# Causal attention of two layers: scores and value products in one rotation of four PSUM banks, value products in two stretches, score-row banks released head by head

## Chip, cores, metric

One core of one Trainium2 chip. The metric is the device time of one execution in microseconds. Engines are called TensorE (PE in the profile; PEld is its weight load), VectorE (DVE), ScalarE (ACT), GpSimd (POOL) and SyncE (SP).

## What is computed

Two transformer layers on x of 4 x 512 x 256, 16 heads of 16 channels. Each layer has a causal attention and a feed-forward part. The change touches the core of the two attentions only, which one function emits for both:

```python
scores = einsum('bqhd,bkhd->bhqk', q, k) * scale     # 4 x 16 x 512 x 512, causal mask
attn = softmax(scores, axis=-1)
out = einsum('bhqk,bkhd->bqhd', attn, v)             # layer 1 shares one k and one v among the heads
```

## The kernel before

`phase_attention` (L705) runs once for each layer, over 16 groups `G`. A group is one batch row and four heads. All matmuls are fp32; the trace shows each as two instructions. For a group there are four kinds of work.

**Row units** (`rows`, L753; VectorE, L816). TensorE computes scores with queries on the partitions, and VectorE reads them from PSUM with the mask added, and reduces them to the negated maximum of each row. A unit `u` of 0 to 5 is one or two query tiles (`ROWS`, L671) of two heads: 512 columns for u = 0 and 3, 256 for u = 1 and 2, 384 + 128 for u = 4 and 5. The two heads have PSUM banks of their own: a pair out of banks 4 to 7, so two pairs rotate (`row_bank`). One semaphore increment for the pair says that it is computed, one that it has been read. In the order of this rotation the maxima's transpose takes a turn of its own, with a whole pair.

**Maxima** (`maxT`, L767; VectorE, L822). TensorE transposes the maxima (four transposes) when the last row unit of the group has been read; VectorE adds them to q. The q_and_max tile is what the next kind reads.

**Transposed scores** (`scoresT`, L737; ScalarE, L838; GpSimd, L851). TensorE computes scores with keys on the partitions, six units of two heads, which are 512, 512, 384 + 128, 384 + 128, 256 and 256 columns a head. ScalarE takes the exponential of each head out of PSUM into the probs tile, GpSimd zeroes the masked half of the diagonal blocks. Heads rotate over three banks, 0 to 2 (`e_bank`): head n waits until head n-3 has been read (L742).

**Value products** (`pv`, L773; ScalarE copy, L829). Four key blocks with 512, 384, 256 and 128 query columns, each with four heads side by side in the output partitions, all in bank 3. The bank is copied once a group.

The order on TensorE is written out by hand (L786 to L801). A group has six steps k = 0 to 5. Step k issues for each of two heads (i = 0, 1) the transposed scores of unit k of group G, and the row unit that is nine units ahead: units 3, 4, 5 of G+1 at k = 0, 1, 2, and units 0, 1, 2 of G+2 at k = 3, 4, 5. The four matmuls of a step use the four 32-row parts of the array, and the columns of both kinds agree at each k. Behind k = 3 stand the transposes for G+1; behind k = 1, 2, 3 and 4 stands one key block each of the value products of G-1 (`PV_AT`). ScalarE copies bank 3 behind the exponentials of k = 5. Each engine works strictly through its own order; a wait holds what stands behind it.

## Time and profile before

| | |
|---|---|
| median of 3 runs | 1081.67 us (1080.73 to 1081.95) |
| span of the profiled execution | 1073.4 us |
| attention core, layer 0 | about 306 to 486 us of the span |
| attention core, layer 1 | about 763 to 943 us of the span |
| busy over the span | PE 86%, DVE 57%, ACT 43%, POOL 27% |

Ends of matmuls are modelled in the profile, so TensorE counts as busy through short waits. What TensorE does is better read from the starts of its instructions in the timeline, one step after the other, and compared with the same step where nothing holds it. "[0.63 <-PE psum L749]" behind a row is the time that the engine had been idle and what released it.

### The profile page before, as it was taken

The page shows a single profiled execution, that of the slowest core. Times are in us where ns is not written, and L with a number is a line of the kernel's source. Part 1 is how long each engine was busy: PE and PEld are TensorE (multiplying, and loading weights), DVE is VectorE, ACT ScalarE, POOL GpSimd, SP SyncE. Part 2 cuts the span into 40 slices and gives each one's busy share as a digit, 9 for nine tenths or more (in the row PEclk, how much of TensorE's full clock was granted, in tenths as well). Part 3 has the DMA queues.
Part 4 walks back from the last instruction along what each step waited for, and adds up shares of the span by engine and source line. Part 5 has one row for each costly group of instructions (what it writes and reads, how often), then busy time and mean ns, then how long its engine had stood idle before and what let it go on. Part 6 is the DMA issues. An engine that isn't in the chain of part 4 may idle for free. (4 is left out here: it accounts for less than half of the span.)

```text
span 1073.4 us, 21548 instructions
## 1 busy us (share of the span) xinstructions
PE 917.8 (86%) x7991; PEld 599.4 (56%) x7991; DVE 610.8 (57%) x2052; ACT 462.5 (43%) x1050; POOL 287.4 (27%) x538
## 2 busy tenths in 40 slices
PE   6865906899969999998999899969899999988874
PEld 3544906777735555546986355534365555467453
DVE  1873794555547777736333635450377777366354
ACT  2563602000005656663232876463256666645054
POOL 1770311455512333330001200000023333340535
PEclk9995556655558999999688999869789999998788
DMA  5055443412200432002000000000000000083461
GB/s 120 4 115 123 133 157 114 95 40 80 62 18 1 95 125 60 2 1 89 1 1 22 6 0 1 1 1 1 1 1 1 2 2 2 1 213 99 160 255 48
DMA packets 54432, 60.42 MB, mean 56 GB/s; under 512 B 9049, under 2 KB 40247, under 8 KB 54072
## 3 DMA queue, kind: packets, MB, share of 16 engines
q1 hardware_dynamic: 43976, 44.31, 15.5%
q10 hardware_dynamic: 7488, 6.85, 2.4%
q0 software_dynamic: 2864, 7.89, 2.1%
q8 instruction: 64, 1.05, 0.4%
q14 instruction: 40, 0.33, 0.1%
HBM read 29.75 MB, written 25.99 MB: 52 GB/s over the span
## 5 line engine op out<-in xcount | busy, mean ns | idle before, releaser
L816 DVE CUSTOM_DVE_ANT_0 l_masked_scores<-psum,mask_q_rows 128x384 bf16<-128x384 f32 (+3 forms) x512 | 225.0, 488 | 77.0 <-PE psum L763 76.2
L838 ACT ACTIVATE l_probs<-psum 128x512 f32<-128x512 f32 (+1 forms) x384 | 186.3, 527 | 150.7 <-PE psum L749 150.0
L851 POOL TENSOR_SCALAR_AFFINE_SELECT l_probs<-l_probs 128x256 f32<-128x256 f32 x256 | 101.0, 406 | 380.9 <-ACT l_probs L838 380.7
L763 PE MATMUL psum<-kb_heads,q_heads 32*128 32x384 f32 (+3 forms) x512 | 109.4, 510 | 10.7 <-DVE l_neg_max_rows L805 8.7
L763 PE MATMUL psum<-l_k_heads,l_q_heads 32*128 32x384 f32 (+3 forms) x512 | 109.4, 509 | 4.6 <-DVE l_neg_max_rows L805 2.7
L749 PE MATMUL psum<-l_q_and_max,l_k_heads 32*128 32x256 f32 (+3 forms) x512 | 112.4, 472 | 0.0
L749 PE MATMUL psum<-l_q_and_max,kb_heads 32*128 32x256 f32 (+3 forms) x512 | 112.3, 472 | 0.0
L781 PE MATMUL psum<-l_probs,rows_32k 128*32 128x512 f32 (+3 forms) x1024 | 97.6, 459 | 2.9 <-POOL l_probs L851 2.9
L749 PEld LDWEIGHTS psum<-l_q_and_max,l_k_heads 32*128 32x128 f32 x512 | 59.0, 188 | 52.0 <-ACT l_probs L838 42.4
L749 PEld LDWEIGHTS psum<-l_q_and_max,kb_heads 32*128 32x128 f32 x512 | 58.9, 188 | 52.0 <-ACT l_probs L838 42.3
L641 POOL TENSOR_TENSOR v_new_and_ones<-v_and_k_rows 32x128 f32<-32x128 f32 x128 | 54.8, 445 | 49.7 <-DVE v_and_k_rows L618 46.0
L763 PEld LDWEIGHTS psum<-kb_heads,q_heads 32*128 32x128 f32 x512 | 53.4, 199 | 21.0 <-DVE l_neg_max_rows L805 8.9
L590 PE MATMUL psum<-eye_and_state,kT 32*128 32x64 f32 x1024 | 62.6, 416 | 2.5 <-PEq L46 1.5
L763 PEld LDWEIGHTS psum<-l_k_heads,l_q_heads 32*128 32x128 f32 x512 | 53.3, 198 | 15.6 <-DVE l_neg_max_rows L816 6.3
L618 DVE TENSOR_TENSOR v_and_k_rows<-psum,own_columns 128x512 f32<-128x512 f32 x64 | 44.2, 691 | 30.4 <-PE psum L590 30.4
L590 PEld LDWEIGHTS psum<-eye_and_state,kT 32*128 32x128 f32 x1024 | 56.7, 317 | 8.0 <-issue 7.9
L838 ACT ACT_TABLE_LOAD x2 | 2.6, 1283 | 115.9 <-PEq L46 115.9
L456 PE MATMUL psum<-rows_32k,v_and_k_rows 128*32 128x128 f32 x448 | 18.5, 339 | 35.5 <-DMA rows_32k<-inverse_scratch 35.5
L597 PE MATMUL psum<-v_and_k_rows,kb_slot_rows 128*32 128x64 f32 x992 | 40.1, 311 | 6.5 <-DVE v_and_k_rows L618 6.5
L816 DVE DVE_READ_ACCUMULATOR2_ANT l_neg_max_rows<- 128x1 f32 x512 | 42.5, 83 | 0.0
L1970 POOL TENSOR_TENSOR x_rows<-x_rows,last_gamma_beta 128x256 f32<-128x256 f32 x16 | 11.6, 727 | 114.0 <-PE psum L1656 114.0
L781 PEld LDWEIGHTS psum<-l_probs,rows_32k 128*32 128x32 f32 x1024 | 21.8, 110 | 31.7 <-issue 19.2
(351 smaller groups left out, 1704.2 us busy)
## 6 DMA issues: line engine op xcount, KB each, us to landing
...
```

Of the source, the lines that this page charges most:

```text
L456: last = nc.tensor.matmul(ps[SLOT * j:SLOT * j + SLOT, u % 4, (2 * cc + q) * P:(2 * cc + q + 1) * P], g.VK[:, u % NP * 2 + cc, 4 * (2 * x ...
L590: last = nc.tensor.matmul(ps[:, 4 * f + j, WB * q:WB * (q + 1)], UW[r, 2 * f + q, c, :], IS[r, f, q, :, :].rearrange("p b e -> p (b e)"), ...
L597: last = nc.tensor.matmul(ps[SLOT * j:SLOT * j + SLOT, 4 * f, 2 * WB + WB * q:2 * WB + WB * (q + 1)], g.KBP[:, c, 4 * (2 * f + q) + j, :], ...
L618: nc.vector.tensor_tensor(VA[:, s % NV, f, :, :, :, :].rearrange("p j q b e -> p j q (b e)"), ps[:, 4 * f:4 * f + 4, 0:2 * WB].rearrange(" ...
L641: last = nc.gpsimd.tensor_tensor(out[:, f, :, :, :], v0, v1, ALU.add)
L749: mm = nc.tensor.matmul(ps[:, e_bank(G, u, i), o:o + w], KT(b, gq)[r, kb * P:(kb + 1) * P], QM[r, G % 2, kb * P:N], start=True, stop=True)
L763: mm = nc.tensor.matmul(ps[:, row_bank(G, u, i), o:o + w], QT(b, gq)[r, t * P:(t + 1) * P], KT(b, gq)[r, 0:w], start=True, stop=True)
L781: last = nc.tensor.matmul(ps[SLOT * j:SLOT * j + SLOT, PV_BANK, kb * P:N], va(b, kb, 4 * gq + j), PT[:, G % 2, j, o:o + w], start=(kb == 0 ...
L816: last = nc.vector.tensor_tensor_reduce(out=junk[:, ROW_AT[G, u] % 2, i, o:o + w], in0=ps[:, row_bank(G, u, i), o:o + w], in1=g.maskq[:, N ...
L838: nc.scalar.activation(PT[:, G % 2, 2 * (u % 2) + i, o:o + w], ps[:, e_bank(G, u, i), 0:w], ACT.Exp, scale=SCALE).then_inc(x_ok, 1)
L851: last = nc.gpsimd.affine_select(out=d, in_=d, pattern=[[0, 2], [1, P]], compare_op=ALU.is_ge, fill=0.0, base=0, channel_multiplier=-1)
L1970: nc.gpsimd.tensor_tensor(g.X[:, c, :], g.X[:, c, :], g.gb_last[:, 1, :], ALU.add).then_inc(xb_ok, 1)
```

## The change

- `row_bank`: each head of a row unit has its own turn in a rotation of four banks, and its own increments on both semaphores. A head waits for the read of the fourth turn before it. The transposes take one turn, not two. VectorE goes head by head.
- `e_bank`: the score heads and the value products share a rotation of four banks, 0 to 3. A group has 14 turns: k0 (two), k1 (two), value product 0, k2, k3, value product 1, k4, k5. Each waits for the read of the fourth turn before it.
- `pv`: two stretches, by query halves. The first, behind k = 1, has queries 0 to 255 (256 and 128 columns of key blocks 0 and 1). The second, behind k = 3 and the transposes, has queries 256 to 511 (256, 256, 256 and 128 columns of the key blocks 0 to 3). That makes six blocks in place of four, with the same sum of 1280 columns a head. The first waits for the masks of four units only, the second for all six.
- The ScalarE copy is two copies of 256 columns, each right behind the exponentials of k = 1 and of k = 3.
- The nine row units that run ahead of group 0 stand in one loop; the transposes of group 0 come behind the sixth, not the seventh.

```diff
--- before.py
+++ after.py
@@ -671,22 +671,37 @@
 ROWS = [[(3, 0)], [(1, 0)], [(1, 0)], [(3, 0)], [(2, 0), (0, 384)], [(2, 0), (0, 384)]]
 UNITS = 6
 PTW = 1280
-PV_AT = {1: [(0, 0)], 2: [(1, 512)], 3: [(2, 1024)], 4: [(3, 896)]}
-
-
-def row_units(G, k):
-
-    n = (G + 1, k + 3) if k < 3 else (G + 2, k - 3)
-    return [n] if 0 <= n[0] < NGRP else []
-
-
-ROW_ORDER = []
-for _G in range(-2, NGRP):
+PT_AT = [0, 512, 1024, 896]
+PV_TURNS = [(1, 0, 256), (3, 256, 512)]
+LEAD = 9
+MAXT_AT = 3
+PV_NEEDS = [max(u for u in range(UNITS) for kb, _ in KEYS[u // 2] if kb * P < q1) + 1 for _, q0, q1 in PV_TURNS]
+
+
+def row_unit(n):
+
+    return [(n // UNITS, n % UNITS)] if n < UNITS * NGRP else []
+
+
+SCORE_AT, ROW_AT, UNIT_AT = {}, {}, {}
+for _n in range(LEAD):
+    for _i in range(2):
+        ROW_AT[_n // UNITS, _n % UNITS, _i] = len(ROW_AT)
+    if _n == UNITS - 1:
+        ROW_AT[0, UNITS, 0] = len(ROW_AT)
+for _G in range(NGRP):
     for _k in range(UNITS):
-        ROW_ORDER += row_units(_G, _k)
-        if _k == 3 and 0 <= _G + 1 < NGRP:
-            ROW_ORDER.append((_G + 1, UNITS))
-ROW_AT = {n: i for i, n in enumerate(ROW_ORDER)}
+        for _i in range(2):
+            SCORE_AT[_G, _k, _i] = len(SCORE_AT)
+            for _H, _u in row_unit(LEAD + UNITS * _G + _k):
+                ROW_AT[_H, _u, _i] = len(ROW_AT)
+        if _k == MAXT_AT and _G + 1 < NGRP:
+            ROW_AT[_G + 1, UNITS, 0] = len(ROW_AT)
+        for _x, _t in enumerate(PV_TURNS):
+            if _t[0] == _k and _G:
+                SCORE_AT[_G - 1, UNITS, _x] = len(SCORE_AT)
+for _x in range(len(PV_TURNS)):
+    SCORE_AT[NGRP - 1, UNITS, _x] = len(SCORE_AT)
 
 
 def load_heads(eng, g, b):
@@ -711,17 +726,16 @@
...
-        junk = sb("masked_scores", [P, 2, 2, N], BF16)
-        zero_ok, row_ps, row_ok = sem("max_rows_zeroed"), sem("score_rows_psum"), sem("row_unit_done")
-        e_ps, x_ok, p_ok, pv_ok, ot_sb = (sem("scoresT_psum"), sem("exponentials"), sem("masked_probs"), sem("pv_done"), sem("out_group_sbuf"))
+        junk = sb("masked_scores", [P, 4, N], BF16)
+        zero_ok, row_ps, row_ok = sem("max_rows_zeroed"), sem("score_rows_psum"), sem("score_rows_read")
+        e_ps, x_ok, p_ok, pv_ok = sem("scoresT_psum"), sem("score_bank_read"), sem("masked_probs"), sem("pv_done")
         block = ctx.enter_context(nc.Block())
-        PV_BANK = 3
 
         def e_bank(G, u, i):
-            return (2 * UNITS * G + 2 * u + i) % 3
+            return SCORE_AT[G, u, i] % 4
 
         def row_bank(G, u, i):
-            return 4 + 2 * (ROW_AT[G, u] % 2) + i
+            return 4 + ROW_AT[G, u, i] % 4
 
...
-                n = 2 * UNITS * G + 2 * u + i
                 if part == 0:
-                    if n >= 3:
-                        pe.wait_ge(x_ok, n - 2)
+                    if SCORE_AT[G, u, i] >= 4:
+                        pe.wait_ge(x_ok, SCORE_AT[G, u, i] - 3)
                     if u == 0 and i == 0:
-                        pe.wait_ge(row_ok, ROW_AT[G, UNITS] + 1)
+                        pe.wait_ge(row_ok, ROW_AT[G, UNITS, 0] + 1)
...
             def rows(G, u, i, part):
                 b, gq, j = G // HG, G % HG, 2 * (u % 2) + i
-                if part == 0 and i == 0:
-                    if ROW_AT[G, u] >= 2:
-                        pe.wait_ge(row_ok, ROW_AT[G, u] - 1)
-                    if streamed and u == 0 and gq == 0:
+                if part == 0:
+                    if ROW_AT[G, u, i] >= 4:
+                        pe.wait_ge(row_ok, ROW_AT[G, u, i] - 3)
+                    if streamed and u == 0 and i == 0 and gq == 0:
                         pe.wait_ge(g.heads_ld[b], 16 * (5 if b else 6))
...
-                if part == len(ROWS[u]) - 1 and i == 1:
+                if part == len(ROWS[u]) - 1:
                     mm.then_inc(row_ps, 1)
 
             def maxT(G):
-                pe.wait_ge(row_ok, max(ROW_AT[G, UNITS] - 1, ROW_AT[G, UNITS - 1] + 1))
+                pe.wait_ge(row_ok, max(ROW_AT[G, UNITS, 0] - 3, ROW_AT[G, UNITS - 1, 1] + 1))
                 for t in range(4):
                     last = nc.tensor.transpose(ps[:, row_bank(G, UNITS, 0), t * P:(t + 1) * P], mx[:, G % 2, t, :], g.idf[:, :])
                 last.then_inc(row_ps, 1)
 
-            def pv(G, kb, o):
+            def pv(G, x):
                 b, gq = G // HG, G % HG
-                if kb == 0:
-                    pe.wait_ge(p_ok, 2 * UNITS * (G + 1))
-                    if G:
-                        pe.wait_ge(ot_sb, G)
-                w = N - kb * P
-                for j in range(4):
-                    last = nc.tensor.matmul(ps[SLOT * j:SLOT * j + SLOT, PV_BANK, kb * P:N], va(b, kb, 4 * gq + j), PT[:, G % 2, j, o:o + w], start=(kb == 0), stop=(kb == 3))
-                if kb == 3:
-                    last.then_inc(pv_ok, 1)
+                _, q0, q1 = PV_TURNS[x]
+                pe.wait_ge(p_ok, 2 * UNITS * G + 2 * PV_NEEDS[x])
+                pe.wait_ge(x_ok, SCORE_AT[G, UNITS, x] - 3)
+                blocks = [kb for kb in range(4) if kb * P < q1]
+                for kb in blocks:
+                    lo = max(q0, kb * P)
+                    o = PT_AT[kb] - kb * P
+                    for j in range(4):
+                        last = nc.tensor.matmul(ps[SLOT * j:SLOT * j + SLOT, e_bank(G, UNITS, x), lo:q1], va(b, kb, 4 * gq + j), PT[:, G % 2, j, o + lo:o + q1],
+                                                start=(kb == 0), stop=(kb == blocks[-1]))
+                last.then_inc(pv_ok, 1)
+
+            def step(S, row):
+                for part in range(2):
+                    for i in range(2):
+                        for G, u in S:
+                            if part < len(KEYS[u // 2]):
+                                scoresT(G, u, i, part)
+                        for G, u in row:
+                            if part < len(ROWS[u]):
+                                rows(G, u, i, part)
 
             pe.wait_ge(zero_ok, 1)
-            for G in range(-2, NGRP):
+            for n in range(LEAD):
+                step([], row_unit(n))
+                if n == UNITS - 1:
+                    maxT(0)
+            for G in range(NGRP):
                 for k in range(UNITS):
-                    for part in range(2):
-                        for i in range(2):
-                            if G >= 0 and part < len(KEYS[k // 2]):
-                                scoresT(G, k, i, part)
-                            for rG, ru in row_units(G, k):
-                                if part < len(ROWS[ru]):
-                                    rows(rG, ru, i, part)
-                    if k == 3 and 0 <= G + 1 < NGRP:
+                    step([(G, k)], row_unit(LEAD + UNITS * G + k))
+                    if k == MAXT_AT and G + 1 < NGRP:
                         maxT(G + 1)
-                    for kb, o in PV_AT.get(k, []):
-                        if G >= 1:
-                            pv(G - 1, kb, o)
-            for kb, o in ((0, 0), (1, 512), (2, 1024), (3, 896)):
-                pv(NGRP - 1, kb, o)
+                    for x, turn in enumerate(PV_TURNS):
+                        if turn[0] == k and G:
+                            pv(G - 1, x)
+            for x in range(len(PV_TURNS)):
+                pv(NGRP - 1, x)
 
         @block.vector
         def _(dve):
             nc.vector.memset(mx[:, :, :, :], 0.0).then_inc(zero_ok, 1)
             dve.wait_ge(zero_ok, 1)
-            for n, (G, u) in enumerate(ROW_ORDER):
+            for n, (G, u, i) in enumerate(ROW_AT):
                 b, gq = G // HG, G % HG
                 dve.wait_ge(row_ps, n + 1)
                 if u < UNITS:
-                    h0 = 2 * (u % 2)
+                    c = SLOT * (2 * (u % 2) + i) + max_row
                     for t, o in ROWS[u]:
                         w = (t + 1) * P
-                        for i in range(2):
-                            out = mx[:, G % 2, t, SLOT * (h0 + i) + max_row:SLOT * (h0 + i) + max_row + 1]
-                            last = nc.vector.tensor_tensor_reduce(out=junk[:, ROW_AT[G, u] % 2, i, o:o + w], in0=ps[:, row_bank(G, u, i), o:o + w], in1=g.maskq[:, N - w:N], scale=-1.0,
-                                                                  scalar=3.0e38, op0=ALU.add, op1=ALU.min, accum_out=out)
+                        last = nc.vector.tensor_tensor_reduce(out=junk[:, n % 4, o:o + w], in0=ps[:, row_bank(G, u, i), o:o + w], in1=g.maskq[:, N - w:N], scale=-1.0,
+                                                              scalar=3.0e38, op0=ALU.add, op1=ALU.min, accum_out=mx[:, G % 2, t, c:c + 1])
                     last.then_inc(row_ok, 1)
                 else:
                     if G >= 2:
@@ -823,22 +844,18 @@
 
         @block.scalar
         def _(act):
-            def out_group(G):
+            for n, (G, u, i) in enumerate(SCORE_AT):
                 b, gq = G // HG, G % HG
-                act.wait_ge(pv_ok, G + 1)
-                nc.scalar.copy(OT[:, gq, :, R * b:R * b + R], ps[:, PV_BANK, :].rearrange("p (c i) -> p c i", c=NT)).then_inc(ot_sb, 1)
-
-            for G in range(NGRP):
-                for u in range(UNITS):
-                    for i in range(2):
-                        act.wait_ge(e_ps, 2 * UNITS * G + 2 * u + i + 1)
-                        if u == 0 and i == 0 and G >= 2:
-                            act.wait_ge(pv_ok, G - 1)
-                        o, w = SPAN[u // 2]
-                        nc.scalar.activation(PT[:, G % 2, 2 * (u % 2) + i, o:o + w], ps[:, e_bank(G, u, i), 0:w], ACT.Exp, scale=SCALE).then_inc(x_ok, 1)
-                    if u == 5 and G:
-                        out_group(G - 1)
-            out_group(NGRP - 1)
+                if u < UNITS:
+                    act.wait_ge(e_ps, 2 * UNITS * G + 2 * u + i + 1)
+                    if u == 0 and i == 0 and G >= 2:
+                        act.wait_ge(pv_ok, len(PV_TURNS) * (G - 1))
+                    o, w = SPAN[u // 2]
+                    nc.scalar.activation(PT[:, G % 2, 2 * (u % 2) + i, o:o + w], ps[:, e_bank(G, u, i), 0:w], ACT.Exp, scale=SCALE).then_inc(x_ok, 1)
+                else:
+                    _, q0, q1 = PV_TURNS[i]
+                    act.wait_ge(pv_ok, len(PV_TURNS) * G + i + 1)
+                    nc.scalar.copy(OT[:, gq, q0 // R:q1 // R, R * b:R * b + R], ps[:, e_bank(G, UNITS, i), q0:q1].rearrange("p (c i) -> p c i", i=R)).then_inc(x_ok, 1)
 
         @block.gpsimd
         def _(pool):
@@ -846,7 +863,7 @@
                 for u in range(UNITS):
                     for part, (kb, o) in enumerate(KEYS[u // 2]):
                         if part == 0:
-                            pool.wait_ge(x_ok, 2 * UNITS * G + 2 * u + 2)
+                            pool.wait_ge(x_ok, SCORE_AT[G, u, 1] + 1)
                         d = PT[:, G % 2, 2 * (u % 2):2 * (u % 2) + 2, o:o + P]
                         last = nc.gpsimd.affine_select(out=d, in_=d, pattern=[[0, 2], [1, P]], compare_op=ALU.is_ge, fill=0.0, base=0, channel_multiplier=-1)
                     last.then_inc(p_ok, 2)
```

## Rows read from the trace of the kernel before

**Rows 1.** Adds of maxima to q of layer 0: min/median/max ns, first and last start (us).
```profile
L822 DVE TENSOR_TENSOR l_q_and_max<-q_heads,psum x16: 681/682/689, 319.9 to 468.7; 128x512 f32<-128x512 f32 x16
```

**Rows 2.** Busy time by window: each engine's busy us (instructions), granted clock, DMA share, GB/s.
```profile
440.00:450.00 10.00, 10.00 (x104) 5.53 (x103) 7.78 (x34) 6.19 (x13) 3.26 (x10) 1.00 0.00 0
```

**Rows 3.** Timeline, TensorE, one period: start, duration in us, line, out<-in, shape, count.
```profile
440.44 0.43 PE L781 MATMUL psum<-l_probs,rows_32k 128*32 128x128 f32 x8
440.80 0.48 PE L749 MATMUL psum<-l_q_and_max,kb_heads 32*128 32x256 f32 x1
...
441.34 0.59 PE L749 MATMUL psum<-l_q_and_max,kb_heads 32*128 32x512 f32 x1
...
441.97 0.69 PE L749 MATMUL psum<-l_q_and_max,kb_heads 32*128 32x512 f32 x1
...
442.46 0.58 PE L763 MATMUL psum<-kb_heads,q_heads 32*128 32x384 f32 x1
...
443.22 0.69 PE L749 MATMUL psum<-l_q_and_max,kb_heads 32*128 32x512 f32 x1
...
444.29 1.06 PE L781 MATMUL psum<-l_probs,rows_32k 128*32 128x512 f32 x8
445.28 0.59 PE L749 MATMUL psum<-l_q_and_max,kb_heads 32*128 32x384 f32 x1
...
446.36 0.85 PE L781 MATMUL psum<-l_probs,rows_32k 128*32 128x384 f32 x8
447.14 0.59 PE L749 MATMUL psum<-l_q_and_max,kb_heads 32*128 32x384 f32 x1
...
448.22 0.66 PE L770 MATMUL psum<-identity,l_neg_max_rows 128*128 128x128 f32 x4
448.80 0.64 PE L781 MATMUL psum<-l_probs,rows_32k 128*32 128x256 f32 x8
449.37 0.69 PE L749 MATMUL psum<-l_q_and_max,kb_heads 32*128 32x256 f32 x2
449.71 0.48 PE L763 MATMUL psum<-kb_heads,q_heads 32*128 32x256 f32 x1
```

**Rows 4.** Timeline, ScalarE, the same period.
```profile
441.53 0.66 ACT L838 ACTIVATE l_probs<-psum 128x256 f32<-128x256 f32 x2 [0.59 <-PE psum L749]
442.07 0.59 ACT L829 COPY l_heads_out<-psum 128x512 f32<-128x512 f32 x1
442.54 1.67 ACT L838 ACTIVATE l_probs<-psum 128x512 f32<-128x512 f32 x3
```

**Rows 5.** Timeline, VectorE, the same period.
```profile
440.60 0.42 DVE L816 CUSTOM_DVE_ANT_0 l_masked_scores<-psum,mask_q_rows 128x256 bf16<-128x256 f32 x1 [0.25 <-PE psum L763]
...
441.29 0.08 DVE L816 DVE_READ_ACCUMULATOR2_ANT l_neg_max_rows<- 128x1 f32 x1
...
446.55 0.56 DVE L816 CUSTOM_DVE_ANT_0 l_masked_scores<-psum,mask_q_rows 128x384 bf16<-128x384 f32 x1 [0.63 <-PE psum L763]
...
447.93 0.08 DVE L816 DVE_READ_ACCUMULATOR2_ANT l_neg_max_rows<- 128x1 f32 x1
...
449.57 0.08 DVE L816 DVE_READ_ACCUMULATOR2_ANT l_neg_max_rows<- 128x1 f32 x1
```

**Rows 6.** Timeline, TensorE, the last group of layer 0.
```profile
470.15 3.54 PE L749 MATMUL psum<-l_q_and_max,kb_heads 32*128 32x256 f32 x12
...
481.28 3.94 PE L781 MATMUL psum<-l_probs,rows_32k 128*32 128x512 f32 x28 [1.31 <-POOL l_probs L851]
```

**Rows 7.** Busy time and granted clock of one window in the tail of layer 0.
```profile
482.00:483.00 1.00, 1.00 (x12) 0.36 (x8) 0.00 (x0) 0.00 (x0) 0.00 (x0) 0.50 0.09 16
```

**Rows 8.** Timeline, ScalarE, the last copy of layer 0.
```profile
485.39 0.58 ACT L829 COPY l_heads_out<-psum 128x512 f32<-128x512 f32 x1 [4.26 <-PE psum L781]
```

**Rows 9.** Timeline, TensorE, the start of layer 0's attention.
```profile
318.64 1.12 PE L770 MATMUL psum<-identity,l_neg_max_rows 128*128 128x128 f32 x4
...
321.67 1.06 PE L749 MATMUL psum<-l_q_and_max,kb_heads 32*128 32x512 f32 x1
```

## The prediction

> **What bounds the kernel now.** I read the table of line groups first, for which engine waits for which, then the busy time of one window, then the timeline of one whole period engine by engine. The program repeats itself: the adds of the maxima to q run from 319.9 to 468.7 us, 16 of them, 9.92 us apart [rows 1]. Layer 1 has the same shape, so the two attentions are 32 groups, some 318 us. In a window of 10 us at full clock VectorE is busy for 7.78 us and ScalarE for 6.19 [rows 2]. Neither fills the period, and TensorE's "busy" hides its waits, so its starts must be compared step by step.
>
> The starts in order give these lengths [rows 3]: value block of 128 columns 0.36, k5 0.54, k0 1.16 (441.34 to some 442.5), k1 1.8, value block of 512 columns 0.99, k2 1.08, block of 384 columns 0.78, k3 1.08, transposes 0.58, block of 256 columns 0.57, k4 0.97. The sum is 9.90. Three of them are longer than the work in them:
> - The second head of k0 starts at 441.97, 0.6 behind the first. With three banks it waits for the exponential of k5's first head, which started at 441.53 [rows 4].
> - The second head of k1 starts at 443.22, when the exponential of k0's first head is read. That one stood behind the 512-column copy of 442.07 and ran from 442.54, 0.59 long [rows 4].
> - k4 is issued at 449.37, but its row matmul starts at 449.71. It waits for VectorE's last read of the pair of k3, which ended at 449.65 [rows 5]; the transposes' turn had taken the other pair of banks. From the end of a read to the start of what it frees, then, 0.06.
>
> So the period is bound by no engine but by rounds from TensorE to ScalarE or VectorE and back, through too few banks.
>
> **What the change does to each term.**
>
> *Value products.* Four stretches of 128, 256, 384 and 512 columns take 0.36, 0.57, 0.78 and 0.99 [rows 3]: 0.21 for each 128 columns and 0.15 once a stretch. The new first stretch has 384 columns: 0.78. The second has 896: 7 x 0.21 + 0.15 = 1.62. Together 2.40 for 2.70. The eight more block matmuls of a group are costed at nothing, since the four heads' loads lie beside streaming matmuls. If each of the two added blocks pays the 0.15 of a stretch again it is 0.3 more a group, which is the bound from above.
>
> *ScalarE.* The exponential of a head may now be read up to four turns later, and the copy is half as wide (0.38 at most, as two 256-column exponentials take 0.66 [rows 4]) and stands behind k1 and k3. For k0 only the exponentials of k4 are needed. The first starts 0.73 after its matmuls (440.80 to 441.53), the second ends 0.66 later [rows 3, 4], with 0.06 for the release 1.45 after the start of k4. k4 and k5 back to back take 2 x 0.54 = 1.08. ScalarE would hold k0's second head for 0.37, less than VectorE does below. k1 needs the exponentials of k5, done before k0's first head has streamed. ScalarE leaves the path.
>
> *Row banks at k4.* The transposes take one turn. k4's heads need the reads of k2's second head and of k3's first, long done. The 0.34 of k4 goes.
>
> *Row banks at k0.* Here a wait comes in. Before, a value block stood between k4 and k5 and covered VectorE; now k4, k5 and k0 stand back to back, and k0's second head needs the read of k4's second head. k4's row matmuls start at 439.81 (449.71 less one period), VectorE starts on them at 440.60, 0.79 later, and has read both heads at 441.37, 0.77 later [rows 5]. A boundary between two units costs about 0.05 on VectorE now; going head by head adds such a boundary (taken as 0.05, bounds 0 and 0.1). With the release: 0.79 + 0.77 + 0.05 + 0.06 = 1.67 after the start of k4. TensorE is there at 1.08. The wait is **0.59**. What is queued behind it on TensorE is k1 and the first value stretch. k1's second head follows its forerunner in k0 by what one head takes, 1.03 (the head released at 441.43 is followed at 442.46 [rows 3, 5]), and the value stretch follows 1.07 behind that (443.22 to 444.29).
>
> *The transposes.* A second wait comes in. They need VectorE's reads of both heads of k2. Before, a value block of 0.78 lay between k2 and k3 and was their cover; now k2, k3 and the transposes stand back to back. VectorE starts on k2's rows 1.27 after the start of k2 (445.28 to 446.55), and its last read ends at 448.01, 1.46 later [rows 3, 5]. With 0.05 and 0.06 the transposes may start 2.84 after k2; TensorE is there at 2 x 1.08 = 2.16. The wait is **0.68**. Behind it stand the long value stretch, k4 and k5, which need nothing from it. VectorE is not late for k2: k1's rows take it 1.46 like k2's, k0's less, and there are 3.3 between the first head of k0 and k2 and 1.27 more.
>
> *The new period*, once around TensorE: k4 to k0's second head 1.67, to k1's second head 1.03, to the value stretch 1.07, that 0.78, k2 to the transposes 2.84, transposes 0.58, value stretch 1.62. **9.59** against 9.90, so 0.31 less. Without the two waits it would be 8.32. Fourteen groups of a layer are of this kind: 28 x 0.31 = 8.7 us.
>
> *The last group* has no rows, so neither wait of VectorE. From the start of k5 before it to the end of its own k5 it is now 470.15 to 479.97 (481.28 less an idle time of 1.31 [rows 6]), 9.82 us. After: 0.54 + 0.37 + 1.03 + 1.07 + 0.78 + 2.16 + 1.62 + 0.54 + 0.70 (a last step with its results) = 8.81. 1.0 less in each layer.
>
> *The tail.* Now all four blocks wait for the last mask. They start at 481.28, the clock granted is 0.50 of full (1.2 GHz) within them [rows 7], and the copy is done at 485.97 [rows 8]: 4.69 us. After, the first stretch runs while ScalarE and GpSimd finish, and only 896 columns and a half copy stand behind the mask: 1.62 + 0.1 + 0.38 = 2.1 at full clock, 3.6 at half. TensorE is idle for about 0.5 us less than before ahead of it, so I take full clock: 2.5 less in each layer, with 1.1 as the other end.
>
> *The start.* The transposes of group 0 come one row step earlier, so of the 3.0 us between them and the first transposed score [rows 9] one 512-column row step more stands behind them. 512 columns are 4 x 0.21 at full clock and twice that at half, so up to 1.7 more. Releases by single heads shorten the row steps before, where VectorE idles; from the 0.6 between heads up to 1.3 back. I take zero, from -1.3 to +1.7 in each layer.
>
> *Sum.* 8.7 + 2 x (1.0 + 2.5) = 15.7 us. The profiled execution spans 1073.4 us, 8.3 under the median; its new span is 1057.7, the time **1066** us.
>
> *A rule against it.* Row matmuls get six more semaphore increments a group. What hides them here is that transposed scores already have one for each head, and that the results of both heads are read one after the other. The Trainium skill (TensorE: Matmul & The Clock Gate, "The cost: per-tile semaphore tail") says that increments of concurrent tiles serialize, at about 26 ns each. By it an estimated 0.05 more stands in each of the two rounds, and the time would be 1069. No row of this trace separates it.
>
> **Rivals.**
> - *The waits are smaller than I price them.* A head's bank is given back after its own read, so TensorE may already load and stream the first head of a step while the second waits, and my chain of second heads may lose less than 0.59. For it: before, the two heads of k0 and k1 ran 0.6 apart and k1 did overlap k0. Against it: the value stretch behind k1 waits for both. With half of both waits gone, a period of 8.95: 28 x 0.95 + 7 = 34, so 1048 us.
> - *The new waits take all.* The added blocks pay 0.15 each and VectorE goes slower head by head (0.1 for a boundary); the period is 9.59 + 0.3 + 0.1, as before. Only the ends gain: 1075 us.
> - *Slower: the clock.* The wait before the transposes leaves the array idle for 0.68 in each group, where now the longest full stop of the two shown is about 0.2 (441.97 + 1.03 to 443.22 [rows 3]). In the tail the clock was at half after a stop of 1.31 [rows 6, 7]. If the clock fell after each transposes' wait, the value stretch would take 1.5 more and k4 and k5 0.85 more, 2.3 a group; in all groups 1130 us. It decides from 8 groups of 28 on (15.7 + 2.2 over 2.3). Against it: the stop is half of that in the tail, with dense work on both sides, and the clock is 1.00 in all full windows now.
>
> **How the numbers follow.** Forecast 0.55 (1060 to 1072), smaller waits 0.16, waits that take all 0.18, slower 0.11 by the clock or by a wait of this kind longer than 1.2. The range reaches half way into the fast case and over the third: 1047 to 1079. Some 0.2% can be told from no change, 2 us. The third case ends within that one time in four. Faster 0.84, within 0.05, slower 0.11.
>
> **What would show it.** In the profile after: adds of maxima 9.6 apart; no stop between k4's scores and rows; the second head of k0 about 0.6 behind where k5 ends, released by VectorE; transposes released by VectorE 2.84 after k2, and not by the end of k3; stretches of 0.78 and 1.62; exponentials that no longer hold TensorE; the last value stretch at full clock. It is wrong if the period is bound by ScalarE, if the stretches are longer, or if the granted clock falls inside groups.

## The result and the profile after

The changed kernel takes 1044.18 us (median of four runs, 1041.61 to 1046.53), the kernel before 1081.62 on the same chip (1080.73 to 1081.95). The ratio is 0.967, interval 0.964 to 0.970: 37 us less. The forecast of 1066 had the sign right and the size wrong; 1044 lies just under the range.

The profiled execution of the changed kernel spans 1043.1 us (1044.79 timed), 30.3 less than the 1073.4 of before. Where it went, each stretch read from first to last instruction, us per attention (layer 0 / layer 1):

| | before | after | saved, both | forecast |
|---|---|---|---|---|
| start of the attention to the first add of maxima | 13.7 / 13.6 | 12.8 / 12.5 | 2.0 | 0 |
| 15 periods between the 16 adds | 148.8 / 148.9 | 139.5 / 140.0 | 18.2 | 8.7 |
| last add to the first matmul of the next stage | 18.0 / 18.2 | 14.4 / 14.7 | 7.1 | 7.0 |
| whole attention | 180.5 / 180.7 | 166.7 / 167.2 | 27.3 | 15.7 |
| everything outside the two | 712.3 | 709.2 | 3.1 | 0 |

The adds of the maxima to q, grouped by line, give the period; the two numbers behind "686, " and "687, " are the first and last start in each layer:

```profile
L843 DVE TENSOR_TENSOR l_q_and_max<-q_heads,psum x16: 682/682/686, 318.1 to 457.6; 128x512 f32<-128x512 f32 x16
L843 DVE TENSOR_TENSOR l_q_and_max<-l_q_heads,psum x16: 681/682/687, 759.4 to 899.4; 128x512 f32<-128x512 f32 x16
```

(457.6 - 318.1) / 15 = 9.30 us, against 9.92 [rows 1]. This mean takes in the first two gaps and the last, which differ; each of the twelve between them is 9.27 here and 9.90 before. Below, "adds ... apart" is the mean of all 15 gaps, and "period" is one of the twelve. Three line groups of the page of the changed kernel show what happened to the two other engines: us busy and mean ns of one, then the idle time ahead of them and its main cause.

```profile
L837 DVE CUSTOM_DVE_ANT_0 l_masked_scores<-psum,mask_q_rows 128x128 bf16<-128x128 f32 (+3 forms) x512 | 220.0, 488 | 60.2 <-PE psum L776 60.2
L854 ACT ACTIVATE l_probs<-psum 128x512 f32<-128x512 f32 (+1 forms) x384 | 171.7, 530 | 75.9 <-PE psum L762 75.8
...
L858 ACT COPY l_heads_out<-psum 128x256 f32<-128x256 f32 x64 | 23.9, 374 | 59.1 <-PE psum L796 57.7
```

ScalarE's exponentials waited 150.7 us for scores before and wait 75.9 now; its copies waited 8.7 for value products and wait 59.1, so a good part of the waiting only moved to the copies. The row reads of VectorE (L837) waited 77.0 and wait 60.2. Which engine holds TensorE is read from the timeline.

One period of TensorE, from the timeline of the changed kernel (start, length, line, form, in brackets idle time and who ended it). L762 are transposed scores, L776 row scores, L783 the transposes of maxima, L796 value products:

```profile
419.84 0.66 PE L783 MATMUL psum<-identity,l_neg_max_rows 128*128 128x128 f32 x4 [0.71 <-DVE l_neg_max_rows L837]
420.43 1.72 PE L796 MATMUL psum<-l_probs,rows_32k 128*32 128x256 f32 x32
422.08 0.48 PE L762 MATMUL psum<-l_q_and_max,kb_heads 32*128 32x256 f32 x1
...
423.52 0.69 PE L762 MATMUL psum<-l_q_and_max,kb_heads 32*128 32x512 f32 x1
423.69 0.69 PE L776 MATMUL psum<-kb_heads,q_heads 32*128 32x512 f32 x1
...
424.65 0.67 PE L762 MATMUL psum<-l_q_and_max,kb_heads 32*128 32x512 f32 x2
...
425.08 0.59 PE L762 MATMUL psum<-l_q_and_max,kb_heads 32*128 32x512 f32 x1
...
425.60 0.86 PE L796 MATMUL psum<-l_probs,rows_32k 128*32 128x256 f32 x16
426.38 0.58 PE L762 MATMUL psum<-l_q_and_max,kb_heads 32*128 32x384 f32 x1
...
429.11 0.66 PE L783 MATMUL psum<-identity,l_neg_max_rows 128*128 128x128 f32 x4 [0.71 <-DVE l_neg_max_rows L837]
```

And the reads of VectorE that stand behind them:

```profile
422.85 0.42 DVE L837 CUSTOM_DVE_ANT_0 l_masked_scores<-psum,mask_q_rows 128x256 bf16<-128x256 f32 x1 [1.25 <-PE psum L776]
...
423.55 0.08 DVE L837 DVE_READ_ACCUMULATOR2_ANT l_neg_max_rows<- 128x1 f32 x1
...
427.59 0.56 DVE L837 CUSTOM_DVE_ANT_0 l_masked_scores<-psum,mask_q_rows 128x384 bf16<-128x384 f32 x1 [0.36 <-PE psum L776]
...
428.97 0.08 DVE L837 DVE_READ_ACCUMULATOR2_ANT l_neg_max_rows<- 128x1 f32 x1
```

Both new waits are there. The transposes at 429.11 come 0.71 idle after k3, when the last read of k2's second head is done (428.97 + 0.08 = 429.05). The second head of k0 issues its rows at 423.69, when the last read of k4's second head is done (423.55 + 0.08 = 423.63), with its bank the one released. ScalarE still holds the scores of k0's second head: they are issued at 423.52, as soon as the exponential of k4's second head has read its bank, 1.44 after k4 (the forecast had 1.45). VectorE's hold ends 0.17 later and is the one that counts. So ScalarE is close behind: by these rows a faster VectorE at this place alone would gain an estimated 0.17 a period at most. The forecast's terms beside these rows:

| once around TensorE | forecast | measured | from |
|---|---|---|---|
| k4 to rows of k0's second head | 1.67 | 1.61 | 422.08, 423.69 |
| that to the first value stretch | 1.03 + 1.07 | 1.91 | 423.69, 425.60 |
| first stretch | 0.78 | 0.78 | 425.60, 426.38 |
| k2 to transposes | 2.84 | 2.73 | 426.38, 429.11 |
| transposes | 0.58 | 0.59 | 419.84, 420.43 |
| second stretch | 1.62 | 1.65 | 420.43, 422.08 |
| sum | 9.59 | 9.27 | |

In the tail, the last value stretch and the copy behind it (timeline), and one window (columns: window, length, busy us and count on TensorE, its loads, VectorE, ScalarE, GpSimd, then granted clock, DMA share, GB/s):

```profile
469.11 1.72 PE L796 MATMUL psum<-l_probs,rows_32k 128*32 128x256 f32 x32 [0.41 <-POOL l_probs L868]
470.90 0.37 ACT L858 COPY l_heads_out<-psum 128x256 f32<-128x256 f32 x1 [1.77 <-PE psum L796]
```

```profile
469.00:470.00 1.00, 0.89 (x16) 0.55 (x20) 0.00 (x0) 0.12 (x1) 0.06 (x1) 1.00 0.06 16
```

The last stretch starts after 0.41 of idle (0.70 in layer 1), runs at full clock and takes 1.7; before, the blocks started after 1.31 of idle and fell to half clock [rows 6, 7].

### The profile page after: what moved, and what is told of

The parts are those of the page before. It is cut to its first block and busy times, and to the rows that moved or that the text cites. A ratio compares the mean times of both kernels' runs of the same rounds, so it can differ in the third digit from the quotient of the medians.

```text
span 1043.1 us, 22638 instructions
## 1 busy us (share of the span) xinstructions
PE 862.9 (83%) x8503; PEld 611.2 (59%) x8503; DVE 605.0 (58%) x2052; ACT 459.4 (44%) x1082; POOL 288.2 (28%) x538
## 5 line engine op out<-in xcount | busy, mean ns | idle before, releaser
L837 DVE CUSTOM_DVE_ANT_0 l_masked_scores<-psum,mask_q_rows 128x128 bf16<-128x128 f32 (+3 forms) x512 | 220.0, 488 | 60.2 <-PE psum L776 60.2
L854 ACT ACTIVATE l_probs<-psum 128x512 f32<-128x512 f32 (+1 forms) x384 | 171.7, 530 | 75.9 <-PE psum L762 75.8
L776 PE MATMUL psum<-kb_heads,q_heads 32*128 32x384 f32 (+3 forms) x512 | 93.5, 488 | 10.4 <-DVE l_neg_max_rows L828 8.7
L776 PE MATMUL psum<-l_k_heads,l_q_heads 32*128 32x384 f32 (+3 forms) x512 | 93.8, 492 | 4.4 <-DVE l_neg_max_rows L828 2.7
L762 PE MATMUL psum<-l_q_and_max,l_k_heads 32*128 32x384 f32 (+3 forms) x512 | 91.6, 462 | 0.0
L762 PE MATMUL psum<-l_q_and_max,kb_heads 32*128 32x384 f32 (+3 forms) x512 | 90.9, 457 | 0.0
L796 PE MATMUL psum<-l_probs,rows_32k 128*32 128x256 f32 (+1 forms) x1536 | 82.5, 347 | 1.1 <-POOL l_probs L868 1.1
L776 PEld LDWEIGHTS psum<-kb_heads,q_heads 32*128 32x128 f32 x512 | 58.9, 197 | 18.0 <-DVE l_neg_max_rows L828 8.9
L776 PEld LDWEIGHTS psum<-l_k_heads,l_q_heads 32*128 32x128 f32 x512 | 59.5, 198 | 12.0 <-DVE l_neg_max_rows L837 3.9
L762 PEld LDWEIGHTS psum<-l_q_and_max,l_k_heads 32*128 32x128 f32 x512 | 56.1, 189 | 17.8 <-issue 6.1
L796 PEld LDWEIGHTS psum<-l_probs,rows_32k 128*32 128x32 f32 x1536 | 43.6, 109 | 38.5 <-issue 8.5
L762 PEld LDWEIGHTS psum<-l_q_and_max,kb_heads 32*128 32x128 f32 x512 | 54.9, 186 | 17.8 <-issue 6.0
L858 ACT COPY l_heads_out<-psum 128x256 f32<-128x256 f32 x64 | 23.9, 374 | 59.1 <-PE psum L796 57.7
L837 DVE DVE_READ_ACCUMULATOR2_ANT l_neg_max_rows<- 128x1 f32 x512 | 42.6, 83 | 0.0
```

Source lines behind the costliest of these rows:

```text
L762: mm = nc.tensor.matmul(ps[:, e_bank(G, u, i), o:o + w], KT(b, gq)[r, kb * P:(kb + 1) * P], QM[r, G % 2, kb * P:N], start=True, stop=True)
L776: mm = nc.tensor.matmul(ps[:, row_bank(G, u, i), o:o + w], QT(b, gq)[r, t * P:(t + 1) * P], KT(b, gq)[r, 0:w], start=True, stop=True)
L796: last = nc.tensor.matmul(ps[SLOT * j:SLOT * j + SLOT, e_bank(G, UNITS, x), lo:q1], va(b, kb, 4 * gq + j), PT[:, G % 2, j, o + lo:o + q1], ...
L837: last = nc.vector.tensor_tensor_reduce(out=junk[:, n % 4, o:o + w], in0=ps[:, row_bank(G, u, i), o:o + w], in1=g.maskq[:, N - w:N], scale ...
L854: nc.scalar.activation(PT[:, G % 2, 2 * (u % 2) + i, o:o + w], ps[:, e_bank(G, u, i), 0:w], ACT.Exp, scale=SCALE).then_inc(x_ok, 1)
L858: nc.scalar.copy(OT[:, gq, q0 // R:q1 // R, R * b:R * b + R], ps[:, e_bank(G, UNITS, i), q0:q1].rearrange("p (c i) -> p c i", i=R)).then_i ...
```

## The experiments

My theory after the result: the period is closed by two rounds from TensorE to VectorE and back, k4 to k0 and k2 to the transposes, and only the head times inside them were priced too high. Rivals: the row banks alone give the gain; the score banks alone do; VectorE's sheer load (7.7 us in a period of 9.3) is the limit; the gain comes from smaller stretches and not from the shared banks; the clock.

**Both kernels once more**, for the spread between executions.

> The kernel before, profiled once more. Its medians lie 37.4 us above those of the changed kernel, the two profiled spans only 30.3 apart (1073.4 and 1043.1), while in the changed kernel time less span is 1.7. Theory: the first profiled execution of before was a short one by some 6 us, outside the attentions, and a new profile spans 1078 to 1080 with the same period of 9.9 us in the attentions. Rival: the difference is in the attentions, and the adds of the maxima lie more than 9.92 us apart here.

> The changed kernel once more, on the same chip as the others of this call: period 9.27 us, each attention 166.7 to 167.3 us from its first VectorE instruction to the next stage's first matmul; the time anywhere from 1036 to 1047, since the stages outside the attentions differ by several us between executions and chips.

Kernel before: median 1079.03 of ten (1065.62 to 1084.09), ratio 1.0012 (0.9967 to 1.0057). Its profile spans 1077.1 where the first one spanned 1073.4. The period is 9.90 again, layer 1 takes 180.6, and the rest, everything outside the two attentions, 711.3 (712.3 in the first profile). Layer 0 takes 185.2 instead of 180.5: from its last add to the next stage it is 23.3, not 18.0. So the time between the two profiles does not lie outside the attentions, as was expected, but in the last group of layer 0. TensorE there, in the first profile and then in this one:

```profile
473.63 1.07 PE L781 MATMUL psum<-l_probs,rows_32k 128*32 128x512 f32 x8
```

```profile
474.55 1.79 PE L781 MATMUL psum<-l_probs,rows_32k 128*32 128x512 f32 x8
...
487.00 4.50 PE L781 MATMUL psum<-l_probs,rows_32k 128*32 128x512 f32 x32 [1.31 <-POOL l_probs L851]
```

The granted clock falls to 0.50 at some 475 us, within the last group, while in the first profile it fell at 481 us, where the last value products start. Nothing in the order of the work differs.

The changed kernel: 1044.62, ratio 0.9655 (0.9581 to 0.9729), period 9.27, attentions 167.1 and 166.2 (expected were 166.7 to 167.3; the start of layer 1 is 0.7 shorter), rest 709.1. Its tails repeat to 0.01 us.

**The row banks by heads, alone.** The kernel before with its row banks given and taken back head by head; score banks, value products and order as before (its waits and increments by heads are left out here).

```diff
-            ROW_ORDER.append((_G + 1, UNITS))
+            ROW_ORDER.append((_G + 1, UNITS, 0))
-            return 4 + 2 * (ROW_AT[G, u] % 2) + i
+            return 4 + ROW_AT[G, u, i] % 4
```

> Before, with only the row banks given back head by head (the transposes take one turn). Theory: only the wait of 0.34 us at k4 goes, since the two other waits are for ScalarE; the period falls from 9.90 to about 9.55, some 0.9 less at each start: 1081.6 - 28 x 0.35 - 2 = about 1070. Rival (what holds one head holds all; ScalarE's waits take up whatever the rows give): period 9.85 or more, time within 3 us of before.

1059.68 us, ratio 0.9836 (0.9785 to 0.9887). Adds 9.49 and 9.52 apart. The period is 9.57, 0.33 less, and the wait of k4 that goes was 0.34 [rows 3]: the theory of 9.55 holds. The tail is as before (17.9 and 18.3). The time is 17 us under the kernel before on the same chip (1076.79), where some 12 were expected, so the row banks alone give about half of the saving.

**The other half, alone.** The changed kernel with row banks in pairs again: one release for a unit, and the transposes take a pair's turn (the waits and increments by pairs are left out here).

```diff
-            return 4 + ROW_AT[G, u, i] % 4
+            return 4 + 2 * (ROW_AT[G, u] % 2) + i
```

> The changed kernel, with the row banks as before: pairs, one increment a pair, the transposes with a pair's turn. Theory: the new period of 9.27 us is made by the score banks and the two stretches; rows by pairs delay k0's first head to 1.67 us after k4 too, but the second follows without a gap, so the period is 9.3 to 9.4 and the time 1046 to 1050. Rival (the release by heads carries the gain that the forecast missed): period 9.6 as forecast, 1053 to 1056.

1054.14 us, ratio 0.9792 (0.9726 to 0.9858). The tail is 14.4 and 14.7, as in the changed kernel: the tail belongs to the value stretches. The timeline of one period, TensorE:

```profile
421.12 0.58 PE L761 MATMUL psum<-l_q_and_max,kb_heads 32*128 32x384 f32 x1
...
426.14 0.48 PE L761 MATMUL psum<-l_q_and_max,kb_heads 32*128 32x256 f32 x1
...
427.31 0.69 PE L761 MATMUL psum<-l_q_and_max,kb_heads 32*128 32x512 f32 x1
427.81 0.69 PE L775 MATMUL psum<-kb_heads,q_heads 32*128 32x512 f32 x1
...
430.52 0.58 PE L761 MATMUL psum<-l_q_and_max,kb_heads 32*128 32x384 f32 x1
```

Period 430.52 - 421.12 = 9.40. Here k0 (its first scores at 427.31) has both row heads behind the read of both heads of k4: rows at 427.81, 1.67 after k4 at 426.14. In the changed kernel only the second head waits, at 1.61, while the first is already streaming. The period was expected at 9.3 to 9.4 and found at 9.40; the time was expected at 1046 to 1050 and missed. Off the period: 0.33 by the rows alone, 0.50 by the rest alone, 0.63 by both. They don't add: in the changed order the transposes and the long stretch stand before k4, and k4's rows follow its scores at once with pairs too (426.14 and 426.15), so both halves take away the same 0.34 of k4; on top of the rest, heads in place of pairs give 0.13.

**Is VectorE's read of k2 on the path, or its load?** One more read of VectorE, 0.48 us of work on constants in SBUF whose result nobody uses, once between the two reads of k2's rows, once at another place of the same period, behind the add of the maxima.

```diff
# dve_more_k2, in the loop over row heads
+                    if u == 5 and i == 1:
+                        nc.vector.tensor_tensor_reduce(out=spare[:, :], in0=g.maskq[:, 0:384], in1=g.maskq[:, 0:384], ...)
# dve_more_idle, behind the add to q
+                    nc.vector.tensor_tensor_reduce(out=spare[:, :], in0=g.maskq[:, 0:384], in1=g.maskq[:, 0:384], ...)
```

> The changed kernel with one more 384-column read and reduction on VectorE (of a constant in SBUF, its result unused) in each group, ahead of the last reads of k2's second head: about 0.48 us. Theory (the transposes wait for these reads): period 9.27 + 0.48 = 9.75. Rival (VectorE has 1.5 us of slack a period and the wait is hidden in the array's streaming): 9.27 to 9.35.

> The same additional read, but behind the add of the maxima to q, where VectorE then waits for k4's rows for 1.2 us. Theory: period unchanged at 9.27. Rival (VectorE's own load binds): 9.75 as in the other place.

1056.64 and 1045.57 us (one run each). With the read in k2 the adds are 9.81 apart and the period is 9.75, 0.48 more than 9.27, as expected. Timeline of VectorE, then of TensorE, from that kernel:

```profile
425.72 0.55 DVE L837 CUSTOM_DVE_ANT_0 l_spare<-mask_q_rows 128x384 bf16<-128x384 f32 x1
...
426.89 0.08 DVE L840 DVE_READ_ACCUMULATOR2_ANT l_neg_max_rows<- 128x1 f32 x1
```

```profile
427.03 0.66 PE L784 MATMUL psum<-identity,l_neg_max_rows 128*128 128x128 f32 x4 [1.19 <-DVE l_neg_max_rows L840]
```

The spare read runs at 425.72, the last read of k2 ends at 426.97, and the transposes start at 427.03 after 1.19 of idle instead of 0.71. With the same work behind the add, VectorE's timeline of the other kernel:

```profile
420.29 0.56 DVE L838 CUSTOM_DVE_ANT_0 l_masked_scores<-psum,mask_q_rows 128x384 bf16<-128x384 f32 x1 [0.36 <-PE psum L777]
...
423.50 0.55 DVE L845 CUSTOM_DVE_ANT_0 l_spare<-mask_q_rows 128x384 bf16<-128x384 f32 x1
...
424.83 0.42 DVE L838 CUSTOM_DVE_ANT_0 l_masked_scores<-psum,mask_q_rows 128x256 bf16<-128x256 f32 x1 [0.77 <-PE psum L777]
...
429.56 0.56 DVE L838 CUSTOM_DVE_ANT_0 l_masked_scores<-psum,mask_q_rows 128x384 bf16<-128x384 f32 x1 [0.36 <-PE psum L777]
```

From k2's first read to the next, 429.56 - 420.29 = 9.27, as without it: the wait before k4's reads (424.83) shrank from 1.25 to 0.77 and took all of it. The same 0.48 costs 0.48 in one place and nothing in the other. (The adds are 9.37 apart there in the mean, since the second of the 15 gaps grew by 0.5.) VectorE's load is not the limit, and its round at k2 is. That its round at k4 is one too is read from the starts and from the moves below; no read was added there.

**Moving the value stretches.** If a round is what counts, a stretch put into it should cover it. Four placements, all by two numbers:

```diff
-PV_TURNS = [(1, 0, 256), (3, 256, 512)]
+PV_TURNS = [(1, 0, 256), (4, 256, 512)]   # pv_k1_k4
+PV_TURNS = [(2, 0, 256), (3, 256, 512)]   # pv_k2_k3
+PV_TURNS = [(2, 0, 256), (4, 256, 512)]   # pv_k2_k4
+PV_TURNS = [(1, 0, 256), (4, 256, 512)]   # max_k4_pv_k4, with
+MAXT_AT = 4
```

> The changed kernel with the second value stretch behind k4, not behind the transposes. Theory of two waits for VectorE on the path: the stretch of 1.65 us now covers VectorE's reads of k4, the wait of 0.5 us at k0 goes (0.1 may come back at k5 or k1), the wait of 0.7 before the transposes stays: period 8.8 to 8.9, 1044 - 28 x 0.4 = about 1033. Rival (the array's own streaming binds, waits are hidden in it): period within 0.1 of 9.27, time within 3 us of the changed kernel.

1044.26 us, ratio 0.9682 (0.9627 to 0.9738); adds 9.16. The long stretch now lies between k4 and k5 and covers VectorE's reads of k4. TensorE and the read that ends its new wait:

```profile
423.86 0.48 PE L762 MATMUL psum<-l_q_and_max,kb_heads 32*128 32x256 f32 x1
...
425.46 0.60 PE L776 MATMUL psum<-kb_heads,q_heads 32*128 32x384 f32 x2
```

```profile
425.33 0.08 DVE L837 DVE_READ_ACCUMULATOR2_ANT l_neg_max_rows<- 128x1 f32 x1
```

k5 starts at 423.86. Now k5, k0 and k1 stand back to back, and k1's second head needs the read of k5's second head, which ends at 425.41: its rows go at 425.46, 1.60 after k5. The wait moved by one step. The forecast of 8.8 to 8.9 had missed it; the period is 9.07, 0.2 less than the changed kernel's. The time is not less (1033 was expected): the attentions are 165.1 and 165.3, 3.5 us less together, but the rest of the profiled execution is 717.2 where the changed kernel had 709.2.

> The changed kernel with the first value stretch behind k2, not k1. Theory: the stretch of 0.79 us covers VectorE's reads of k2, so the wait of 0.7 before the transposes goes; but k2 then follows k1 at once and its second head needs the read of k0's, some 0.3 later than it could start: period about 8.9, transposes released by the end of k3 and not by VectorE. Rival (no wait before the transposes is on the path): period 9.27 or more.

Adds 9.03 apart, one run, 1045.21 us. TensorE:

```profile
419.09 0.48 PE L762 MATMUL psum<-l_q_and_max,kb_heads 32*128 32x256 f32 x1
...
425.80 0.66 PE L783 MATMUL psum<-identity,l_neg_max_rows 128*128 128x128 f32 x4
...
428.03 0.48 PE L762 MATMUL psum<-l_q_and_max,kb_heads 32*128 32x256 f32 x1
```

With the short stretch between k2 and k3, the transposes follow k3 at 425.80 with no idle time: VectorE reads k2 under the stretch and k3. Period 428.03 - 419.09 = 8.94, 0.33 less than 9.27, as expected. From k2 to the transposes the changed kernel takes 2.73, and k2 and k3 without a stop take 2.16: 0.57 went there, and 0.24 of it came back at k2, which now follows k1 at once.

> The changed kernel with the transposes and the second value stretch both behind k4. Theory (two rounds to VectorE are left on the path): the 0.7 us before the transposes are filled by k4 (0.54 us of work), the round of k4 by the stretch; what stays is VectorE's round from k5 to k1, 1.6 us, as in the run with the stretch behind k4 alone. Sum: k5 to the first stretch 2.66, that 0.79, k2 to the transposes 2.73, transposes 0.59, stretch 1.65: period 8.42, 1044 - 28 x 0.85 = about 1020. Rival (VectorE's or ScalarE's own work binds below 9 us): period 8.9 or more, 1033 or more.

1039.83 us, ratio 0.9649 (0.9576 to 0.9722); adds 9.13 and 9.15. TensorE and the read:

```profile
427.00 0.48 PE L776 MATMUL psum<-kb_heads,q_heads 32*128 32x256 f32 x1
...
427.69 0.48 PE L776 MATMUL psum<-kb_heads,q_heads 32*128 32x256 f32 x1
```

```profile
427.55 0.08 DVE L837 DVE_READ_ACCUMULATOR2_ANT l_neg_max_rows<- 128x1 f32 x1
```

Expected was 8.42, found 9.04. Moving the transposes moves their turn among the four row banks. Now k4's second head gets the bank of k2's second head, whose read ends at 427.63: its rows go at 427.69, 0.69 after the first head's. The read of k2 that held the transposes holds k4 instead: from k2 to the transposes it is 3.35 (424.96 to 428.31) where 2.73 was expected, the whole 0.62.

> The changed kernel with the value stretches behind k2 and k4, the transposes behind k3 as they are: each stretch now stands where VectorE is behind. Theory: no wait before the transposes (as with the stretch behind k2), none of k4 at k0; what stays is VectorE's round from k5 to k1's second head (1.60 us, 0.3 of it waiting) and from k0's reads to k2 (about 0.4). Sum: k5 to the first stretch 4.07, that 0.79, k3 1.07, transposes 0.59, k4 0.65, stretch 1.65: period 8.8, 0.45 under the changed kernel, so about 13 us less than that kernel on the same chip. Rival (the wait moves and grows back, as it did with the transposes behind k4): 9.0 or more.

1043.17 us, ratio 0.9656 (0.9591 to 0.9721); adds 9.12. TensorE, and a read of VectorE:

```profile
420.49 0.48 PE L762 MATMUL psum<-l_q_and_max,kb_heads 32*128 32x256 f32 x1
...
420.75 0.48 PE L776 MATMUL psum<-kb_heads,q_heads 32*128 32x256 f32 x1
...
423.03 0.48 PE L762 MATMUL psum<-l_q_and_max,kb_heads 32*128 32x256 f32 x1
...
427.09 0.86 PE L796 MATMUL psum<-l_probs,rows_32k 128*32 128x256 f32 x16
```

```profile
420.62 0.08 DVE L837 DVE_READ_ACCUMULATOR2_ANT l_neg_max_rows<- 128x1 f32 x1
```

k5 (423.03) to the first stretch (427.09) takes 4.06, as expected. But k4 now follows the transposes with no long stretch between, and its second head has the bank of k3's first head. That read ends at 420.70; the rows go at 420.75, 0.26 after the first head. Expected 8.8, found 9.04.

Its tail is 0.5 longer than the changed kernel's, since the first stretch starts a step later. All four placements end between 8.94 and 9.07. In all four a part of the wait that was removed came back in the next step that takes the bank; in three of them more than was expected.

**Two stretches without the shared rotation.** Scores rotate through three banks and value products keep the fourth, as before; stretches, order and row banks as in the changed kernel.

```diff
-            return SCORE_AT[G, u, i] % 4
+            return 3 if u == UNITS else (2 * UNITS * G + 2 * u + i) % 3
```

> The changed kernel with three banks for the scores and the fourth for the value products alone, as before; stretches, copies and row banks as changed. It tells the shared rotation from the rest. Theory: with three banks ScalarE holds k0's second head until 1.17 us after k5, 0.1 longer than VectorE does, and k1's second head until the exponential of k0's first is read, 0.26 longer: period 9.6. Rival (the gain is in the stretches and rows, since VectorE's waits cover ScalarE's anyway): 9.27 to 9.35.

1073.69 us, adds 10.19 apart, period 10.21: slower in its groups than the kernel before (9.90). TensorE, then ScalarE:

```profile
429.06 0.81 PE L763 MATMUL psum<-l_q_and_max,kb_heads 32*128 32x384 f32 x2
...
429.89 0.58 PE L763 MATMUL psum<-l_q_and_max,kb_heads 32*128 32x384 f32 x1
```

```profile
429.24 1.08 ACT L856 ACTIVATE l_probs<-psum 128x512 f32<-128x512 f32 x2 [0.66 <-PE psum L763]
```

The second head of k3 issues at 429.89, 0.83 behind the first, when the exponential that started at 429.24 has read its bank. With one bank fewer, ScalarE stands on the path again, at k3, k5 and k1. I had expected 9.6 and counted only k5 and k1; three stops add up to more. The fourth bank in the rotation is worth 10.21 - 9.27 = 0.94 us a period in this order, more than the whole gain of 0.63; cutting the value products in two without it loses 0.31 against the kernel before. The time is still under that of the kernel before on the same chip (1078.66), though the attentions are longer (184.2 and 182.0): the rest of its one execution took 705.8.

**The tail.** In the last group alone, both value stretches wait for the last mask.

```diff
-                pe.wait_ge(p_ok, 2 * UNITS * G + 2 * PV_NEEDS[x])
+                pe.wait_ge(p_ok, 2 * UNITS * G + 2 * (UNITS if G == NGRP - 1 else PV_NEEDS[x]))
```

> The changed kernel, but the first value stretch of the last group of each layer also waits for the last mask, as all value products did before. From the last add of the maxima to the next stage it is 14.4 and 14.7 us in the changed kernel, 18.0 and 18.2 before. Theory of the tail (the early stretch saves its own 0.8, and more by keeping the clock up): 2.4 us of matmuls behind the mask at half clock are 4.8, so 14.4 + 0.8 + 2.4 = 17.6. Rival (the clock stays up, only the length counts): 15.2.

1050.36 us. Periods as in the changed kernel. The tail is 15.1 in layer 0 and 17.0 in layer 1, for 14.4 and 14.7: the rival in layer 0 (15.2), near the theory in layer 1 (17.6). TensorE in both, and the window of layer 1:

```profile
471.41 2.37 PE L796 MATMUL psum<-l_probs,rows_32k 128*32 128x256 f32 x48 [1.28 <-POOL l_probs L868]
...
913.76 4.05 PE L796 MATMUL psum<-l_probs,rows_32k 128*32 128x256 f32 x48 [1.57 <-POOL l_probs L868]
```

```profile
915.00:916.00 1.00, 1.00 (x16) 0.49 (x12) 0.00 (x0) 0.33 (x1) 0.00 (x0) 0.50 0.00 0
```

The same 48 block matmuls take 2.37 us after a stop of 1.28, and 4.05 after one of 1.57, with the granted clock at 0.50 (1.2 GHz). So of the 3.6 that the tail and the last group gain in each layer, 0.7 is the first stretch done early, and 1.7 more is the clock where it falls. That the shorter stop is what keeps the clock at full is not shown. In the run with three banks it fell to 0.50 in layer 0 within the last stretch, after a stop of 0.58:

```profile
486.89 3.05 PE L798 MATMUL psum<-l_probs,rows_32k 128*32 128x256 f32 x32 [0.58 <-ACT l_heads_out L860]
```

The same stretch of layer 1, after the same stop of 0.58, ran at full clock in 1.72. And in the second profile of the kernel before it fell at 475 us with no stop of TensorE longer than 0.1 us in the 40 us ahead of it. The length of the last stop alone does not decide it.

## Why the prediction was right and wrong

- *Where the 37 us lie.* The forecast was 15.7, so it is off by 21.7. Of this 11.6 is in the attentions (9.5 in the periods, 2.0 at the start, 0.1 in the tail), 3.1 in what lies outside them, which the forecast put at nothing, and 7.0 in the base (below). With the attentions alone, 27.3 us less, the time would have been 1054. The step of the prediction that failed is the sum for the new period, 9.59 for a measured 9.27; its mechanism stands, and its terms were too large.
- *What bounds it* was right. No engine is full; the old stops of k0, k1 and k4 are gone. ScalarE is off the path by 0.17 only, as the forecast had it (1.44 for 1.45 behind k4).
- *The two new waits* were right in place and cause: 0.71 before the transposes for a forecast of 0.68, and k0's second head released 1.61 after k4 for 1.67. Doing k2's read 0.48 later cost 0.48.
- *The term that failed most: k0 to the first stretch.* I took 1.03 for a head and 1.07 from the head to the stretch, both from rows in which a second head had been held: within the 1.03 (441.43 to 442.46 [rows 3]) ScalarE held k0's second head, and the 1.07 starts at 443.22, where k1's second head was released. With k1's heads following without a stop, 1.91 is what both take, for 2.10. That is 0.19 of the 0.32 a period. Some 0.11 of it shows in k1's second head: its two passes of scores start 0.54 apart in the kernel before (443.22 and the row below) and 0.43 apart here (424.65, 425.08). The other 0.08 no row separates.

```profile
443.76 0.59 PE L749 MATMUL psum<-l_q_and_max,kb_heads 32*128 32x512 f32 x1
```

- *The 0.05 for a boundary between heads on VectorE* was nothing. The two reads of k2 take 1.46 (427.59 to 429.05) as before, those of k4 0.78 for 0.77. And VectorE starts 1.21 after k2, not 1.27: it no longer waits for the second head of the unit. (In the run with pairs in the changed order it starts 1.26 after k2 and 0.84 after k4; by heads 1.21 and 0.77.) Together 0.11 too much in k2's round, 0.06 in k4's. That makes 0.36, and the second stretch gives 0.03 back (1.65 for 1.62).
- *Added blocks at nothing*: right for the first stretch (0.78), and within 0.03 for the second.
- *Rival "smaller waits"* gave 1048, nearest to the result, and its mechanism is partly there: the first head of k0 does stream while the second waits. But the waits are not halved (0.71 for 0.68 before the transposes); the heads behind the release are shorter. That its time lies near the result is in part luck: its period was 8.95 and the measured one is 9.27, and 10 of the 37 us are not in the attentions.
- *The small error, many times.* 0.32 of 9.59 is 3%, but the saving was 0.31 of 9.90. The saving doubled: 0.63 a period, 18.2 for 8.7 in all.
- *The start* gained 2.0 where I took zero, inside the bounds (1.3 back in each layer at most). It comes with the row banks by heads: 12.9 and 12.8 with them alone, 13.5 and 13.3 with the other half alone, 13.7 and 13.6 before.
- *Last group and tail*: 7.1 for a forecast of 7.0, with the clock at full; the agreement is partly luck. In layer 0 the last group gave 0.8 for 1.0, and the stretch with its copy 2.5 for 2.5 (469.11 to 471.27, for 4.69). The stop ahead of it is 0.9 shorter (0.41 for 1.31), which the sum did not have, and some 0.6 goes off because the long stretch now stands behind the last add. Against the second profile of the kernel before, where the clock fell earlier, it would be 5.2 more.
- *The slower rival, the clock.* It didn't come: TensorE stops for 0.71 in each group, and behind the start (0.50 until some 325 us in layer 0 and some 770 in layer 1) the granted clock is 1.00 in every window of the groups.
- *The semaphore rule.* Six more increments a group were to cost an estimated 3 us by the Trainium skill (TensorE: Matmul & The Clock Gate, "The cost: per-tile semaphore tail"). Both rounds came out shorter than priced without it. Nothing here shows the cost. The Trainium skill states it there for concurrent tiles. In this kernel VectorE also starts on the first head of a unit alone, and whether this hides a cost of that size no run tells apart.
- *The base.* I took the 8.3 us between the profiled span and the median as a fixed part around the span. It isn't: each timed execution is its span + 1.7 (1044.79 for 1043.1), and 1073.4 was a low draw among spans whose median is 1076.3 (the four timed executions of the kernel before are others, with spans of some 1079 to 1080 by this rule). The forecast of a difference doesn't hang on it, but it is why 30 us between two profiles stand against 37 between medians.

*What stays open.* The median span is 1076.3 for 27 executions of the kernel before (1077.4 for ten more) and 1042.4 to 1042.9 for the changed one (two sets of four): 34 less. The pair of first profiles has 27.3 of this in the attentions. With the second profile of the kernel before it would be 32, since its last group of layer 0 ran at half clock. How often that happens the times do not tell, so how the remaining 2 to 7 us divide stays open. The mean granted clock of an execution goes with its span: in the 27 it lies between 0.819 and 0.840, and 0.01 more goes with some 8 us less. Its median is 0.829 for the kernel before and 0.837 for the changed one, which by that slope is 6 us. The parts outside the attentions take 711.3 and 712.3 in the two profiles of the kernel before and 709.1 and 709.2 in the two of the changed one, but 705 to 717 over the variants, in code that none of them touches; and three placements with nearly the same order had a lower mean clock (medians 0.829 to 0.834). I don't call a gain outside the attentions shown to be an effect of the change.

*The best of the runs.* By time it was max_k4_pv_k4 with 1039.8 us; its attentions are 164.0 and 164.6, 2.7 less each than in the changed kernel. By the attentions it was pv_k2_k3, 163.1 and 163.3, with the shortest period (8.94), though its one time was 1045.2. Both differences are more than the 0.4 and 1.0 by which the changed kernel's two profiles differ in a layer; 5 us between the medians (1039.8, 1044.6) is not more than the spread of single executions.
